# One Transformer block: attention products in column quarters, work moved from VectorE and ScalarE to GpSimd

## The reference

```
x = x + attention(layernorm(x))          # 16 heads of 8, softmax over 512 keys, head mask, Wo, bo
x = x + moe(layernorm(x))
attention: q, k, v = x @ W.T + b
           a = softmax(q k / sqrt(8)) * head_mask[head];  out = (a @ v) @ Wo.T + bo
moe:       shared = gelu(x @ Wfc_s + bfc_s) @ Wproj_s + bproj_s          # 128 -> 512 -> 128
           top 2 of 8 experts of softmax(x @ Wr), gates renormalised over the two
           out = shared + sum over the two of gate * (gelu(x @ Wfc[e] + bfc[e]) @ Wproj[e] + bproj[e])
```

## Time and profile before

| | before |
|---|---|
| median of 3 runs | 700.45 us (699.07 to 701.12) |
| profiled execution | 700.0 us, span 698.2 us |
| PE busy | 633.9 us, 91% |
| DVE busy | 540.3 us, 77% |
| ACT busy | 437.9 us, 63% |
| POOL busy | 256.6 us, 37% |
| chain that ended last | PE 63%, DVE 14%, issue 7% |

### The profile page before, as it was taken

The page is one execution under the profiler, slowest core; times in us unless marked ns, Lnnn a source line. Parts: engine busy times, 40 slices in busy tenths (PEclk is TensorE's granted clock), DMA queues, the critical chain, the costliest instruction groups (busy, mean ns, idle before and its releaser), DMA issues.

```text
span 698.2 us, 13370 instructions
## 1 busy us (share of the span) xinstructions
PE 633.9 (91%) x3934; PEld 324.6 (46%) x3976; DVE 540.3 (77%) x1180; ACT 437.9 (63%) x953; POOL 256.6 (37%) x386
## 2 busy tenths in 40 slices
PE   1766799999999999999999999997979999999996
PEld 1441222323323323323332332323779999998965
DVE  6998778888998998988989989822656666666558
ACT  0881467777687787787787787793425555555541
POOL 6766200020430420421521512506464555454541
PEclk9996799999999999999999999999999999999998
DMA  5399594411311212212221121000112222212174
GB/s 151 93 335 349 126 237 107 115 46 36 92 44 43 83 43 68 69 45 63 63 64 48 58 69 48 21 1 31 47 50 66 66 65 63 68 59 62 47 246 127
DMA packets 67611, 61.28 MB, mean 88 GB/s; under 512 B 16250, under 2 KB 58106, under 8 KB 67562
## 3 DMA queue, kind: packets, MB, share of 16 engines
q1 hardware_dynamic: 63242, 51.79, 26.7%
q0 software_dynamic: 4320, 8.89, 3.8%
HBM read 35.76 MB, written 24.62 MB: 86 GB/s over the span
## 4 chain that ended last, share of the span: by engine, by line
PE 63%; DVE 14%; issue 7%; SPq 5%; POOL 4%; ACT 4%; DMA 3%; DVEq 0%; ACTq 0%; POOLq 0%; another core or an unknown queue 0%
PE ps L1183 13%; PE ps L1172 13%; PE ps L1154 12%; PE ps L1357 10%; PE ps L1369 8%; DVE mx L827 6%; POOL slots L514 2%; DVE x_sb L1097 2%; SPq L295 2%; DMA q_op<-mxT 2%; PE ps L1309 1%; DVE o_t L835 1%; PE ps L1209 1%; PE ps L1317 1%; SPq L305 1%
## 5 line engine op out<-in xcount | busy, mean ns | idle before, releaser
L676 ACT ACTIVATE probs<-ps 128x512 f32<-128x512 f32 x512 | 278.8, 595 | 102.5 <-PE ps L1172 87.8
L827 DVE TENSOR_REDUCE mx<-ps 128x2 f32<-128x1024 f32 x256 | 304.0, 1212 | 42.8 <-PE ps L1154 37.5
L1154 PE MATMUL ps<-k_op,q_op 96*128 96x512 bf16 x512 | 181.5, 394 | 19.2 <-DVE mx L827 7.0
L1172 PE MATMUL ps<-q_op,k_op 128*128 128x512 bf16 x470 | 179.0, 387 | 2.2 <-DMA q_op<-mxT 1.5
L1172 PEld LDWEIGHTS ps<-q_op,k_op 128*128 128x128 bf16 x512 | 49.6, 98 | 187.5 <-ACT probs L676 127.7
L1183 PE MATMUL ps<-probs,v_op 128*32 128x512 f32 x1024 | 136.0, 604 | 0.5 <-issue 0.2
L723 ACT ACTIVATE probs<-ps,b_cur 128x128 f32<-128x128 f32 x284 | 81.4, 368 | 75.7 <-PE ps L1357 65.3
L577 POOL DMA_INDIRECT results<-rest,row_id x71 | 73.9, 1041 | 75.1 <-DVE rest L1041 57.1
L514 POOL DMA_INDIRECT slots<-route_sb,slot_u x64 | 67.0, 1046 | 75.1 <-ACT probs L676 50.8
L1357 PE MATMUL ps<-xn,qk 128*128 128x128 f32 x568 | 79.2, 284 | 3.7 <-DVE xn L1034 1.7
L1154 PEld LDWEIGHTS ps<-k_op,q_op 96*128 96x128 bf16 x512 | 49.5, 99 | 61.7 <-DVE mx L827 27.6
(11 more groups left out here) (135 smaller groups left out, 591.8 us busy)
## 6 DMA issues: line engine op xcount, KB each, us to landing
q_op<-q_scr SPq DMA_DIRECT2D x96, 96.0 KB
k_op<-k_scr SPq DMA_DIRECT2D x96, 96.0 KB
w_sb<-in_W SPq DMA_DIRECT2D x18, 256.0 KB, 4.0
probs<-slots SPq DMA_DIRECT2D x71, 64.5 KB, 1.9
k_scr<-probs SPq DMA_DIRECT2D x16, 256.0 KB, 3.7
q_scr<-probs SPq DMA_DIRECT2D x8, 384.0 KB, 3.1
k_scr<-probs SPq DMA_DIRECT2D x8, 384.0 KB, 3.6
k_scr<-probs SPq DMA_DIRECT2D x16, 128.0 KB, 3.1
```

Source lines behind the costliest of these rows:

```text
L676: nc.scalar.activation(probs[:, i, j, :], ps[:, BK_S + j % key_banks(b, hg), :], ACT.Exp, scale=float(D) ** -0.5).then_inc(s_exp, 1)
L827: nc.vector.reduce_max(mx[:, slot % 2, 2 * p:2 * p + 2], ps[:, bank:bank + 2, :], AX.X).then_inc(s_max, 1)
L1154: last = nc.tensor.matmul(ps[:, BK_A + a % 4, :], q_op[hg][0:SH, j, P * i:P * (i + 1)], k_op[hg][0:SH, j, :], start=True, stop=True)
L1172: nc.tensor.matmul(ps[:, BK_S + j % key_banks(b, hg), :], k_op[hg][:, j, P * i:P * (i + 1)], q_op[hg][:, j, :], start=True, stop=True).the ...
```

## The change

- Column tiling: row scores, key scores, row-maximum transposes and output projections are made as products of 32 output columns (`QUARTERS`), four to a score, each into its own partition quarter of the same bank. The row-maximum transpose becomes a plain product with the identity that gives 32 rows.
- Order on PE: `ROW_TILES` puts two row scores behind each even key score and none behind the odd ones. `pv` is cut into two halves of 256 columns each, in the slots of `PV_SLOTS`.
- Paired output bank: two groups share bank 6; v of the odd groups stands 16 columns further (`HALF_OUT`), and `out_norm` runs once per two groups on twice the elements. The head mask is multiplied into `wo_sb` once, on POOL, and loaded by one DMA in place of four.
- To POOL: the residual (ACT copies the projection out of PSUM first), the second normalisation (`normalise_y`), counts (`count_rows`) and slots (`find_slots`) as trees of additions. DVE keeps its own forms of these for the last sequence alone.
- To ACT: copies of the logits and of the ranks. The transposed y is copied straight to where it is kept.
- `zero_sb` becomes a view of `fill_sb`, whose memset moves ahead of POOL's third parts.

```diff
-        PV_LAG, MX_STEP, YT_STEP = 11, 7, 13
-        Y_STEPS = (-1, 3, 7, 11)
+        MX_STEP, YT_STEP = 7, 11
+        AP_STEP = -10
+        ROUTER_STEP, LOGITS_STEP = 0, 18
+        RANKS_AT, RANKS_STEP = 13, 31
-        ROW_TILES = ((0,), (1, 2), (3,), ())
+        ROW_TILES = ((0, 1), (), (2, 3), ())
+        PV_SLOTS = ((11, 12, 13, 15, 17, 19, 21, 23), (9, 11, 13, 15, 17, 19, 21, 23))
+        QUARTERS = [slice(32 * c, 32 * c + 32) for c in range(P // 32)]
...
-            nc.gpsimd.memset(v_op[:, :, :, :, 0:1], 1.0).then_inc(s_pad, 1)
-            nc.gpsimd.memset(zero_sb[:, :, :], 0.0).then_inc(s_pad, 1)
+            for hg in range(HG):
+                nc.gpsimd.memset(v_op[:, hg, :, :, HALF_OUT * (hg % 2):HALF_OUT * (hg % 2) + 1], 1.0).then_inc(s_pad, 1)
+            nc.gpsimd.memset(fill_sb[:, :, :, 0:C], 0.0).then_inc(s_pad, 1)
...
+            def normalise_y(b):
+                pool.wait_ge(s_scale, b + 1)
+                wait(pool, s_put, b * (16 * NC))
+                wait(pool, s_yTp, b)
+                for i in range(NT):
+                    last = nc.gpsimd.tensor_scalar(y2[:, i, :, 0:C], x_sb[:, e_tile(b, i), :].unsqueeze(1).to_broadcast([P, K2, C]),
+                                                   rstd[:, i:i + 1], neg_shift[:, i:i + 1], ALU.mult, ALU.add)
+                last.then_inc(s_yn, 1)
...
+            def find_slots(b):
+                pool.wait_ge(s_cn, (b + 1) * Q + 1)
+                pool.wait_ge(s_rk, b + 1)
+                nc.gpsimd.tensor_tensor(run_bf[:, :], run_bf[:, :], seq_n[:, :], ALU.add).then_inc(s_cn, 1)
+                pool.wait_ge(s_rkc, b + 1)
+                nc.gpsimd.tensor_tensor(at_f[:, :, :], at_f[:, :, :], chosen[:, :, :], ALU.mult).then_inc(s_at, 1)
...
-                if b > 0:
-                    ln2_scales(b - 1)
                 gather_v(b, 3)
                 max_split(g + 3)
                 if b > 0:
+                    ln2_scales(b - 1)
+                    normalise_y(b - 1)
                     y_row_ids(b - 1)
...
                 if b > 0:
-                    keep_yT(b - 1)
+                    count_rows(b - 1)
+                    find_slots(b - 1)
...
+            def copy_projection(b):
+                act.wait_ge(s_ap, b + 1)
+                wait(act, s_x2, b)
+                nc.scalar.activation(projected[:, :], ps[:, BK_M, :], ACT.Copy).then_inc(s_apc, 1)
...
-                last = nc.tensor.matmul(ps[:, BK_A + a % 4, :], q_op[hg][0:SH, j, P * i:P * (i + 1)], k_op[hg][0:SH, j, :],
-                                        start=True, stop=True)
+                for c in QUARTERS:
+                    last = nc.tensor.matmul(ps[c, BK_A + a % 4, :], q_op[hg][0:SH, j, P * i + c.start:P * i + c.stop],
+                                            k_op[hg][0:SH, j, :], start=True, stop=True)
...
-                nc.tensor.matmul(ps[:, BK_S + j % key_banks(b, hg), :], k_op[hg][:, j, P * i:P * (i + 1)], q_op[hg][:, j, :],
-                                 start=True, stop=True).then_inc(s_sb, 1)
+                for c in QUARTERS:
+                    last = nc.tensor.matmul(ps[c, BK_S + j % key_banks(b, hg), :],
+                                            k_op[hg][:, j, P * i + c.start:P * i + c.stop], q_op[hg][:, j, :],
+                                            start=True, stop=True)
+                last.then_inc(s_sb, 1)
...
                 for j in range(J):
-                    last = nc.tensor.matmul(ps[32 * j:32 * j + 32, BK_O, :], v_op[:, hg, i, j, :], probs[:, i, j, :],
-                                            start=(i == 0), stop=(i == NT - 1))
-                last.then_inc(s_pv, 1)
+                    last = nc.tensor.matmul(ps[32 * j:32 * j + 32, BK_O, cols], v_op[:, hg, i, j, :], probs[:, i, j, cols],
+                                            start=(hg % 2 == 0 and i == 0 and half == 0),
+                                            stop=(hg % 2 == 1 and i == NT - 1 and half == 1))
+                if half == 1:
+                    last.then_inc(s_pv, 1)
```

More of the change, by code:

```diff
@@ L527, in _ @@
             pool.wait_ge(s_route, 16 * N_ROUTE)
-            nc.gpsimd.memset(fill_sb[:, :, :, 0:C], 0.0)
             nc.gpsimd.tensor_copy(fill_sb[:, :, :, C:ROW].bitcast(u32), dump_sb[:, 0:E, :, :]).then_inc(s_fillrows, 1)
@@ L543, in gather_and_route @@
                         max_split(g + 2)
+                    if n == NC - 1 and b > 0:
+                        residual(b - 1)
                     if b > 1:
                         route_step(b, n)
-                if b > 0:
-                    ln2_scales(b - 1)
                 gather_v(b, 3)
@@ L868, in router_step, with ln2_stats @@
-            def router_step(b, step):
-                if step == 0:
-                    dve.wait_ge(s_lgp, b + 1)
-                    nc.vector.tensor_copy(logits[:, :, :], ps[:, BK_M, 0:NT * E].rearrange("p (n e) -> p n e", e=E)).then_inc(s_rt, 1)
-                elif step == 1:
-                    dve.wait_ge(s_rt, b * R + 1)
+            def ln2_stats(b, half):
+                if half == 0:
+                    dve.wait_ge(s_x2, b + 1)
+                    dve.sem_inc(s_bn, 1)
+                for i in range(NT // 2 * half, NT // 2 * (half + 1)):
+                    last = nc.vector.bn_stats(stats[:, i, :], x_sb[:, e_tile(b, i), :])
+                if half == 1:
+                    last.then_inc(s_st, 1)
@@ L875, in router_step, with copy_logits @@
+            def copy_logits(b):
+                dve.wait_ge(s_lgp, b + 1)
+                nc.vector.tensor_copy(logits[:, :, :], ps[:, BK_M, 0:NT * E].rearrange("p (n e) -> p n e", e=E)).then_inc(s_lgc, 1)
+            def router_step(b, step):
+                half = slice(NT // 2 * (step % 2), NT // 2 * (step % 2 + 1))
+                if step < 2:
+                    if step == 0:
+                        dve.wait_ge(s_lgc, b + 1)
+                        wait(dve, s_gd, b)
                     dve.sem_inc(s_bn, 1)
-                    for i in range(NT):
+                    for i in range(half.start, half.stop):
@@ L877, in router_step @@
                         last = nc.vector.max(top8[:, i, :], logits[:, i, :])
                     last.then_inc(s_rt, 1)
-                elif step == 2:
-                    dve.wait_ge(s_rt, b * R + 2)
-                    nc.vector.tensor_tensor(l_diff[:, bass.ds(b * NT, NT)], top8[:, :, 1], top8[:, :, 0], ALU.subtract).then_inc(s_gd, 1)
-                    for i in range(NT):
+                elif step < 4:
+                    dve.wait_ge(s_rt, b * R + step - 1)
+                    for i in range(half.start, half.stop):
@@ L1207, in project_out @@
                     if last_b:
-                        pe.wait_ge(s_cn, (b + 1) * Q)
-                last = nc.tensor.matmul(ps[:, BK_M, C * i:C * (i + 1)], o_sb[:, P * i:P * (i + 1)], wo_sb[:, :],
-                                        start=True, stop=True)
+                        pe.wait_ge(s_rkc, B - 1)
+                for c in QUARTERS:
+                    last = nc.tensor.matmul(ps[c, BK_M, C * i:C * (i + 1)], o_sb[:, P * i + c.start:P * i + c.stop], wo_sb[:, :],
+                                            start=True, stop=True)
                 if i == NT - 1:
```

232 lines of the change are left out of this document (131 added, 101 removed).

## The result

The changed kernel took **691.85 us** (median of 4, 690.44 to 693.40), the kernel before on the same chip 700.21: ratio 0.988, with an interval of 0.987 to 0.990. Forecast were 671 us and a ratio of 0.958. The saving is 8.4 us, not 29.1. So there are two questions: what was lost on the chip of the result alone, and what the forecast missed on every chip.

The account below looks back on a forecast made before the run. PE was taken to bound the attention, 49.0 of 50.31 us per sequence. Terms 6 x 4.3 + 2.4 + 2.5 + 0.6 - 1.0 - 1.2 = 29.1 us off 700.0 gave 671 us, own range 663 to 679, with rivals 662 to 690.

Parts of the forecast that it names:

- The 0.22 us is a price of changing the column shape: PE around each PV: 0.22 us per step is lost to the 32-column shape against 128, and goes with one shape.
- Rival C: PE at PV: 0.22 us is paid per start of PV, so halves double it; 717 us, chance 0.04.
- Quarters side by side at full rate: PE's scores: four 32-column products run side by side, so a score still takes 0.218 us.
- rival D: PE's quartered scores: weight loads or issue too slow, +13 us per sequence, about 765 us; chance 0.04.
- Full-width places cost 3 x 0.22: PE's y transposes, router and ranks keep 128 columns; changing shape in and out costs 0.7 us per sequence.
- New waits of 0.8 per sequence: Attention: PE waits 0.4 us for DVE's first-group extras and 0.4 for exps pushed by ACT's copies; period 46.0.
- POOL's slot writes at no cost: Attention, POOL: no term for slot writes; POOL's total of 14.2 + about 7 of 46 us was called no issue.
- POOL's normalisation hidden: Third group: POOL's normalised rows, 0.6 us per operation, ready at 6.3 us, wanted by PE's transposes at 7.9.
- rival B: Third group: POOL's normalisations at 1.26 us each come 1.0 to 1.4 late in seven sequences; 680 us, chance 0.11.
- Last sequence -3.1: Last sequence's attention: groups one and two gain 1.2 + 1.3 us, the others 0.6 without ACT's four normalisations.
- Behind the last exp +1.2: After the attention: slots come by ACT and six POOL operations instead of DVE, delaying POOL's slot writes by 1.2 us.
- Rival A: Attention: two-bank loops bind, waits of 3 us per sequence remain, period 48, 685 us; chance 0.16.

Follow-up runs that it names:

- full_width: Changed kernel with key and row scores as single products of 128 columns again, PV halves and new order kept: 729.36 us, ratio 1.039 to the kernel before.
- earlier_later: Changed kernel with ACT's projection copy two steps earlier and POOL's fill_sb memset behind all third parts: 685.38 us, ratio 0.979 to the kernel before.
- after_again: Changed kernel, unchanged, on another chip, where the kernel before takes 688.74 us: 670.66 us, ratio 0.974.
- before_again: Kernel before, unchanged, run once on a chip where it takes less than in the result: 687.75 us.
- three_moves: earlier_later plus the slots of the last sequence but one found by VectorE straight from PSUM: 659.70 us, ratio 0.958 to the kernel before.
- four_moves: three_moves plus slot writes spaced wider (steps 2, 6, ... 30), on four chips: 658.05 to 660.29 us, ratios 0.954 to 0.959 to the kernel before.
- spare_writes: Changed kernel plus sixteen writes nobody reads in the second sequence, eight by GpSimd, eight by SyncE; five runs on five chips: 666.98 to 672.88 us.

## Why the prediction was wrong, step by step

The forecast saved 29.1 us and the two profiled executions differ by 7.2. Of the 21.9 between them 13.9 lie in the six middle sequences (10.5 from the slot writes, 3.4 from new waits beyond the 0.8 forecast), 3.2 in the last sequence (2.2 from the slot writes), 4.9 behind the last exp and 1.6 ahead of the first; the first sequence gave 1.7 more than forecast.

- **The 0.22 us is a price of changing the column shape: right.** full_width brings it back as 0.23 per visit, and the step fell to 2.60 (forecast 2.62). Rival C (a price per start of PV) falls with the 0.43 per half. The Trainium skill (TensorEngine Tiling (Array Packing), Key Properties) says that a change of tiling mode drains TensorE; the runs agree and put 0.09 ahead of PV and 0.14 behind it.
- **Quarters side by side at full rate: right.** Four in 0.22 for whole groups, so rival D falls. The Trainium skill (TensorE: Matmul & The Clock Gate, Part 3, The mechanism) says that a load overlaps products in flight only where its row group differs. The trace disagrees for 32 columns too: in the fifth sequence a key score's four loads, 0.10 us from 270.36 on, lie beside the half PV that starts at 270.14 and takes 0.43, with 128 rows in both.
- **Full-width places cost 3 x 0.22: right for router and ranks**, 12.03 - 10.46 = 1.57 in the fourth group against 0.79 + 0.3 + 2 x 0.22 = 1.53. In the third, 11.66 - 10.46 = 1.20 against 0.44 + 0.22: PE idles 0.4 more ahead of the y transposes, which the trace puts down to no engine.
- **New waits of 0.8 per sequence: the step that failed on every chip.** The wait for DVE's burst was right (first group 10.75 against 10.46). What was missing: PE's row-maximum transposes wait for ACT's copy of the projection. The order shows both, the transposes and the copy, one step apart; I priced what the copy does to the exps and not who waits for the bank. 0.68 a sequence (earlier_later), 4.8 us over seven. Without it the period is 45.89 against the forecast 46.0.
- **POOL's slot writes at no cost: the step that failed on the chip of the result.** The change leaves them behind the same steps, and the forecast gave them no term in the attention ("the total is no issue"). They cost 2.0 to 2.2 us in each of six sequences, 12 to 13 us in all, where products come in quarters; after minus after_again from first to last exp is 378.4 - 366.2 = 12.2. No trace of before shows it (its first groups are alike with and without slot writes), so it was not to be read off it; but PE with four times the instructions beside GpSimd's DMAs was something that trace doesn't show, and it should have had a bound in the range, or a rival. It had neither.
- **POOL's normalisation hidden: right.** It is ready in time, so rival B falls:

```profile
L502 POOL TENSOR_SCALAR route_sb<-x_sb,rstd,neg_shift 128x256 f32<-128x256 f32 x12 | 6.5, 550 | 0.3
```

  0.55 each (forecast 0.6). In the sequence of these rows the last ends at 300.15, and the y transposes' first load is at 300.77.
- **DVE 41.0, ACT 36.7: low by 1.3 and 2.4.** An exp takes 0.597 when the next doesn't follow at once, 0.54 only in a row of four; nothing hung on it. The double-size normalisation was 0.407, the reciprocal of twice the size 0.331.
- **Before the attention +1.0: 2.64.** The memset's term was right (1.1, see earlier_later). The rest had no term: in these two executions it takes 4.1 us from the end of the shift rows' second issue to the first exp, against 3.1 before, and why is open.
- **First sequence -2.4: -4.1.** Its second group gained 1.6, which I had given to its DMA. In part this is chance: that group takes 12.85 in one execution of before and 11.83 in the other, and after_again is 2.7 below before_again (45.53 and 48.24).
- **Last sequence -3.1: +0.07 with the hold, -2.1 in after_again** (41.2 from its first exp to its last, 43.3 in before). Its third group was to gain from ACT's four normalisations, and lost 0.5 (10.49 from 10.03): the wait for POOL's rows, which the forecast names, takes 1.86 us. In the executions in which the clock falls there the sequence takes 42.9.
- **Behind the last exp +1.2: +6.1.** Slot writes start 3.25 behind the last exp's start, not 0.63:

```profile
458.26 0.41 ACT L713 ACTIVATE at_f<-ps 128x64 f32<-128x64 f32 x1
```

```profile
458.75 0.31 POOL L545 TENSOR_TENSOR at_f<-at_f,chosen 128x64 f32<-128x64 f32 x1 [1.53 <-ACT at_f L713]
...
460.02 0.19 POOL L553 CAST slot_u<-slot_f 128x8 uint32<-128x8 f32 x1
461.04 1.31 POOL L561 DMA_INDIRECT slots<-route_sb,slot_u  x1 [0.83 <-issue]
```

  ACT's copy stands behind all sixteen exps of the last group and six operations follow; before, the first write starts 0.63 behind the last exp's start. This is 2.6, I took 1.2. Then the shared experts' products on the path run at the lower clock (1.2 GHz) in part: chain pieces of after, then of before,

```profile
477.96 5.88 PE ps L1399 x32
```

```profile
487.99 3.57 PE ps L1317 x32
```

  2.3 more, behind a PE that had idled for the slot writes (granted clock 0.5 from 475.8 on, for 6.8 us). Another 1.1 is not traced. three_moves and four_moves, in which VectorE finds these slots, have 216.0 to 216.7 behind the last exp's start where after_again has 221.0: the late slots are worth nearly all of the loss there.
- **Rival A (period 48, waits of 3 us, 685)** comes near by luck, for another reason: the waits are there (48.6 against a floor of 45.2), but with the same two banks the period is 46.56 on a chip without the hold, and 45.89 with the copy two steps earlier. That it and the result still differ by 7 us is mostly the time behind the last exp.

What stays open: why one chip shows the hold and five others do not, by what path a GpSimd write stops PE's hand-over, and whether a plain one does. The Trainium skill (SBUF — State Buffer, SBUF: two separate sides) says that engine ports and DMA ports do not contend; no run here tells whether they are involved.

## What to carry to other kernels

When every product gets one column shape, the price of changing it goes (0.65 us a group here), and this pays for the quarter products; but look at the order of the queue as well, since with PV whole the new order took all of it back, and with the inputs of ACT evenly spaced (and less work on DVE and ACT) a group lost another 0.4 us. When a copy moves to another engine, ask who reuses its source and in which slot that one stands, before asking what the copy pushes back. And time a change of this kind on more than one chip: here the same pair of kernels gave 0.988 and 0.974.

## What the runs showed of the hardware

- Between a product with 128 output columns and one with 32, PE loses 0.09 us going to the 32 and 0.14 coming back (full_width); within one shape nothing is lost between bf16 and f32, 96 and 128 rows, or products of 256 and 512 columns.
- On one chip, and in the result, each GpSimd indirect write of 128 rows holds up TensorE's hand-overs for up to about 1 us from about the end of its instruction on, when products are quartered (2.0 to 4.5 us per eight writes); with full-width bf16 scores it does not. On five other chips it was not seen.
- The chips differ in the expert tiles too, with 71 such writes and full-width f32 products, in both kernels: 227.0 against 216.2 us behind the last exp's start for before, 233.1 against 221.0 for after. That the writes are the cause there was not tested.
- In the last sequence PE's granted clock fell from 1.00 to 0.5 (1.2 GHz) for 3.4 us behind an idle time of 1.86 us in three of the five spare_writes, and not in the other two nor in after and after_again; where it did, the group took 1.3 us longer.
